# Autocorrelation on one core: weights transformed at plain delays, outputs as even and odd parts, and two steps moved

## What is computed

```python
qf, kf = fft(q), fft(k)
corr = ifft(qf * conj(kf)).real
w, idx = top_k(corr, topk)          # topk = int(2 ln 256) = 11
w = softmax(w)
for i in range(topk):
    g = minimum(idx[..., i] + pos, L - 1)
    out += w[..., i] * v[g]         # the context, shifted by the delay, clamped at its last row
```

## Time and profile before

| | |
|---|---|
| median of 3 runs | 2161.8 us (2161.77 to 2164.0) |
| profiled execution, its own time | 2167.1 us |
| profiled execution, span | 2165.1 us |
| mean granted TensorE clock | 0.977 |
| TensorE (PE) busy | 2052.2 us, 95% |
| VectorE (DVE) busy | 1098.7 us, 51% |
| ScalarE (ACT) busy | 1175.9 us, 54% |
| GpSimd (POOL) busy | 663.7 us, 31% |
| tail, from its first instruction | 1600.1 us to 2165.1 us |

### The profile page before, as it was taken

One profiled execution on the slowest core, in us unless ns is written; L12 is line 12 of the kernel. 1 busy time (PEld: TensorE's weight loads), 2 busy tenths in 40 slices (PEclk: granted clock), 3 DMA queues, 4 the chain that ended last, 5 costly groups with the idle time before them and its releaser, 6 DMA issues. The chain is left out here.

```text
span 2165.1 us, 25964 instructions
## 1 busy us (share of the span) xinstructions
PE 2052.2 (95%) x9634; PEld 1023.6 (47%) x9634; DVE 1098.7 (51%) x1951; ACT 1175.9 (54%) x1851; POOL 663.7 (31%) x640
## 2 busy tenths in 40 slices
PE   7985999999999999999999999999975899999997
PEld 5772444444444444444444444444432455555543
DVE  5774252442624335253352524335257788888852
ACT  6993755656566565665656566565613334344321
POOL 3432211112121121211112121121225676667741
PEclk9997999999999999999999999999987899999999
DMA  6632211112122121221221111111130011111000
GB/s 222 201 127 61 77 49 59 48 51 70 58 65 69 55 69 54 69 69 55 64 63 55 49 55 49 55 49 51 44 125 24 12 40 49 49 49 46 13 30 29
DMA packets 64925, 136.76 MB, mean 63 GB/s; under 512 B 8992, under 2 KB 13728, under 8 KB 64800
## 3 DMA queue, kind: packets, MB, share of 16 engines
q1 hardware_dynamic: 64800, 135.11, 19.1%
HBM read 122.49 MB, written 12.58 MB: 62 GB/s over the span
## 5 line engine op out<-in xcount | busy, mean ns | idle before, releaser
L682 ACT ACTIVATE first<-first 128x512 f32<-128x512 int32 x1008 | 632.7, 628 | 28.0
L920 PE MATMUL ps_ring<-xT_hi,gu_hi 128*128 128x512 f16 x1376 | 524.2, 381 | 1.7 <-POOL gu_lo L758 1.7
L920 PE MATMUL ps_ring<-xT_lo,gu_hi 128*128 128x512 f16 x1376 | 523.7, 381 | 0.0
L920 PE MATMUL ps_ring<-xT_hi,gu_lo 128*128 128x512 f16 x1376 | 523.2, 380 | 0.0
L812 DVE SCALAR_TENSOR_TENSOR wt<-first,w_scale,absm 128x512 f32<-128x512 f32 x132 | 98.8, 749 | 478.5 <-ACT first L682 477.4
L758 POOL TENSOR_TENSOR gu_lo<-wt,gu_hi 128x512 f16<-128x512 f32 x88 | 102.6, 1166 | 765.2 <-ACT gu_hi L688 765.2
L831 DVE SCALAR_TENSOR_TENSOR X<-ps_ring,ffn_gain,X 128x512 f32<-128x512 f32 x352 | 259.8, 749 | 135.3 <-PE ps_ring L943 135.3
L943 PE MATMUL ps_ring<-dn_hi,hid_hi 128*128 128x512 f16 x704 | 266.9, 379 | 0.0
L943 PE MATMUL ps_ring<-dn_hi,hid_lo 128*128 128x512 f16 x704 | 266.7, 379 | 0.0
L943 PE MATMUL ps_ring<-dn_lo,hid_hi 128*128 128x512 f16 x672 | 254.6, 379 | 0.0
L920 PEld LDWEIGHTS ps_ring<-xT_hi,gu_hi 128*128 128x128 f16 x1376 | 135.1, 98 | 171.7 <-issue 14.5
(11 more groups left out here) (203 smaller groups left out, 2683.1 us busy)
## 6 DMA issues: line engine op xcount, KB each, us to landing
first<-in_codes SPq DMA_DIRECT2D x132, 256.0 KB, 2.8
absm<-in_absmax SPq DMA_DIRECT2D x264, 128.0 KB, 3.0
X<-in_x SPq DMA_DIRECT2D x16, 512.0 KB, 4.3
c_in<-in_ctx SPq DMA_DIRECT2D x16, 512.0 KB, 5.3
cT<-in_ctxT SPq DMA_DIRECT2D x16, 512.0 KB, 3.6
xT_hi<-in_ctx SPq DMA_DIRECT2D x8, 1024.0 KB, 7.1
out<-X SPq DMA_DIRECT2D x16, 512.0 KB, 2.6
wide<-in_w SPq DMA_DIRECT2D x8, 512.0 KB, 4.7
```

Source lines behind the costliest of these rows:

```text
L682: act.activation(level[u % 2][:], codes[u % RING] if k == 0 else level[u % 2][:], ACT.Prelu, bias=bias, scale=scale, alpha=alpha).then_inc ...
L920: mm = pe.matmul(o[:], w[c][:, m, k, :], xx[:, k, ts], start=(q == 0), stop=(q == 3 * KD - 1))
```

## The change

The weights are no longer folded. `w_fold` goes; ScalarE norms `cut` itself, and both 128-delay halves of it are transposed. The transform matrices of the weights (`delay_hi`, `delay_lo`) take the 256 plain delays, so that each of the four spectra is a sum over both halves. The output is made as a symmetric part in `psQ[:, 0]` and an antisymmetric one in `psQ[:, 1]`. VectorE adds the symmetric part to both rows of X, ScalarE copies the antisymmetric one to SBUF, and GpSimd adds it to one row and subtracts it from the other. The moved steps are TensorE's `turn(nxt, 0)`, now behind `output(n)`, and VectorE's `add(n)`, now ahead of `low(nxt, 0)`. The list of ScalarE changes only where it is shown.

```diff
@@ SyncE, constants (in the feed-forward phase)
-                for name in ("fwd", "fwd_hi", "fwd_lo", "inv"):
+                for name in ("fwd", "fwd_hi", "fwd_lo", "inv", "back", "delay_hi", "delay_lo"):
                     sp.dma_start(res[name], io[name]).then_inc(res["const_in"], 16)
@@ GpSimd
-                def w_fold(n):
-                    if n:
-                        pool.wait_ge(wT_mm, n)
-                    for c in (0, 2):
-                        pool.wait_ge(w_done, CH * n + c + 2)
-                        for k, op in enumerate((ALU.add, ALU.subtract)):
-                            pool.tensor_tensor(wf[:, k, c:c + 2, :], cut[:, c:c + 2, 0:P], cut[:, c:c + 2, P:L][:, :, ::-1], op).then_inc(wf_done, 1)
+                def dc_fix(n):
+
+                    pool.wait_ge(wprod_comb, 4 * n + 1)
+                    pool.tensor_tensor(e_d[0:1, 0, :], e_d[0:1, 0, :], e_d[0:1, 1, :], ALU.subtract).then_inc(dc_done, 1)
+
+                def anti_add(n):
+                    pool.wait_ge(anti_done, n + 1)
+                    for t, op in enumerate((ALU.add, ALU.subtract)):
+                        pool.wait_ge(sym_done, 2 * n + t + 1)
+                        dst = X[:, 2 * (n // 2) + t, cols(n)]
+                        pool.tensor_tensor(dst, dst, anti[:], op).then_inc(x_done, 1)
...
                 for n in range(N + LAG):
                     now = tile(n - LAG)
+                    if 0 < n <= N:
+                        anti_add(n - 1)
                     if n + 1 < N:
                         corr_comb(n + 1)
...
                         out_comb(n, 1)
+                        dc_fix(n)
...
-                    if n + 1 < N:
-                        w_fold(n + 1)
@@ ScalarE
                 def weights(n):
                     act.wait_ge(rws_done, n + 1)
                     for c in range(CH):
-                        act.wait_ge(wf_done, 4 * n + 2 * (c // 2) + 2)
-                        act.activation(wf[:, :, c, :], wf[:, :, c, :], ACT.Copy, scale=rws[:, c:c + 1]).then_inc(wn_done, 1)
+                        act.activation(cut[:, c, :], cut[:, c, :], ACT.Copy, scale=rws[:, c:c + 1]).then_inc(wn_done, 1)
+
+                def anti_out(n):
+                    act.wait_ge(anti_mm, n + 1)
+                    if n:
+                        act.wait_ge(x_done, 2 * n)
+                    act.activation(anti[:], psQ[:, 1, :], ACT.Copy, scale=half_gate[:]).then_inc(anti_done, 1)
...
                         exps(n + 1)
                         odd_out(n + 1)
                         weights(n + 1)
+                    if n < N:
+                        anti_out(n)
                     if n + 2 < N:
                         even_out(n + 2)
@@ TensorE
                 def q_spectrum(n):
                     pe.wait_ge(qlo_done, n + 1)
                     if n >= 2:
-                        pe.wait_ge(x_done, 2 * n - 2)
+                        pe.wait_ge(sym_done, 2 * n - 2)
+                        pe.wait_ge(anti_done, n - 1)
...
+                def weight_spectrum(k):
+                    for half in range(2):
+                        for q, (w, src) in enumerate(((delay_hi, wT_hi), (delay_hi, wT_lo), (delay_lo, wT_hi))):
+                            for h in range(2):
+                                mm = pe.matmul(psE[:, half, :], w[:, 2 * k + half, h, :], src[:, h, :], start=(q + h == 0), stop=(q + h == 3))
+                    mm.then_inc(ws_mm, 1)
 
                 def weight_even(n):
...
-                    for half in range(2):
-                        mm = dft_parts(psE, half, half, wT_hi[:, half, :], wT_lo[:, half, :])
-                    mm.then_inc(ws_mm, 1)
+                    weight_spectrum(0)
...
                 def output(n):
                     pe.wait_ge(prod_done, min(2 * n + 4, 2 * N))
                     pe.wait_ge(wprod_row, n + 1)
-                    for k, src in enumerate((e_d, e_x, n_d, n_x)):
-                        pe.wait_ge(wprod_comb, 4 * n + k + 1)
-                        for t in range(2):
-                            mm = pe.matmul(psQ[:, t, :], inv[:, k, t * P:(t + 1) * P], src[:, 0, :], start=(k == 0), stop=(k == 3))
-                    mm.then_inc(out_mm, 1)
+                    pe.wait_ge(wprod_comb, 4 * n + 2)
+                    pe.matmul(psQ[:, 1, :], back[:, 1, :], e_x[:, 0, :], start=True, stop=False)
+                    pe.wait_ge(wprod_comb, 4 * n + 3)
+                    pe.matmul(psQ[:, 1, :], back[:, 2, :], n_d[:, 0, :], start=False, stop=True).then_inc(anti_mm, 1)
+                    pe.wait_ge(wprod_comb, 4 * n + 4)
+                    pe.matmul(psQ[:, 0, :], back[:, 3, :], n_x[:, 0, :], start=True, stop=False)
+                    pe.wait_ge(dc_done, n + 1)
+                    pe.matmul(psQ[:, 0, :], back[:, 0, :], e_d[:, 0, :], start=False, stop=True).then_inc(out_mm, 1)
...
                         linear(now, 1)
-                    if nxt is not None:
-                        turn(nxt, 0)
                     if n + 1 < N:
                         k_odd(n + 1)
                     if n < N:
                         output(n)
+                    if nxt is not None:
+                        turn(nxt, 0)
                     if n + 2 < N:
                         k_even(n + 2)
@@ VectorE
                     if n:
-                        dve.wait_ge(wf_done, 4 * n)
+                        dve.wait_ge(wT_mm, n)
...
                     for t in range(2):
                         dst = X[:, 2 * (n // 2) + t, cols(n)]
-                        dve.scalar_tensor_tensor(dst, psQ[:, t, :], half_gate[:], dst, ALU.mult, ALU.add).then_inc(x_done, 1)
+                        dve.scalar_tensor_tensor(dst, psQ[:, 0, :], half_gate[:], dst, ALU.mult, ALU.add).then_inc(sym_done, 1)
...
                         gain_of(now, 1)
+                    if n < N:
+                        add(n)
                     if nxt is not None:
                         low(nxt, 0)
-                    if n < N:
-                        add(n)
                     if nxt is not None:
                         low(nxt, 1)
```

More of the change, by code:

```diff
@@ L1015, in spectra @@
     fwd = np.stack([np.cos(even), even_im, np.cos(odd), -np.sin(odd)]).transpose(1, 0, 2)
-    scaled = fwd * DFT_SCALE
-    high = scaled.astype(np.float16)
+    weight = np.where(f == 0, 1.0, 2.0) / L
+    back_im = even_im * weight
+    back_im[:, :1] = np.sin(np.pi * t) / L
+    back = np.stack([np.cos(even) * weight, back_im, np.cos(odd) * 2 / L, -np.sin(odd) * 2 / L]).transpose(2, 0, 1)
     t = np.arange(L)[:, None]
@@ L1020, in spectra @@
     nyquist = np.where(t % 2 == 0, 1.0, -1.0)
-    weight = np.where(f == 0, 1.0, 2.0) / L
     im_inv = -np.sin(even) * weight
     im_inv[:, :1] = (nyquist - 1.0) / L
-    inv = np.stack([np.cos(even) * weight, im_inv, np.cos(odd) * 2 / L, -np.sin(odd) * 2 / L])
-    return fwd.astype(np.float32), high, (scaled - high).astype(np.float16), inv.transpose(2, 0, 1).astype(np.float32)
+    inv = np.stack([np.cos(even) * weight, im_inv]).transpose(2, 0, 1)
+    delay_im = -np.sin(even)
+    delay_im[:, :1] = -nyquist
+    delay = np.stack([np.cos(even), delay_im, np.cos(odd), -np.sin(odd)]).reshape(4, 2, P, P).transpose(2, 0, 1, 3)
+    scaled = [fwd[:, :2] * DFT_SCALE, delay * DFT_SCALE]
+    high = [m.astype(np.float16) for m in scaled]
+    low = [(m - h).astype(np.float16) for m, h in zip(scaled, high)]
+    return {"fwd": fwd.astype(np.float32), "inv": inv.astype(np.float32), "back": back.astype(np.float32),
+            "fwd_hi": high[0], "fwd_lo": low[0], "delay_hi": high[1], "delay_lo": low[1]}
 def phase_tail(nc, io, res):
@@ L1045, in sem @@
             return ctx.enter_context(nc.semaphore("a_" + name))
-        fwd, fwd_hi, fwd_lo, inv, const_in, ctx_in = (res[k] for k in ("fwd", "fwd_hi", "fwd_lo", "inv", "const_in", "ctx_in"))
+        fwd, fwd_hi, fwd_lo, inv, back, delay_hi, delay_lo = (res[k] for k in ("fwd", "fwd_hi", "fwd_lo", "inv", "back", "delay_hi", "delay_lo"))
+        const_in, ctx_in = res["const_in"], res["ctx_in"]
         c_in = [res[f"ctx_in{s}"] for s in range(2)]
@@ L1084, in phase_tail @@
         top_done, cut_done, nmax_done, next_done, fill_done, cut2_done = (sem(n) for n in ("top_done", "cut_done", "nmax_done", "next_done", "fill_done", "cut2_done"))
-        ex_done, w_done, rws_done, wf_done, wn_done = (sem(n) for n in ("ex_done", "w_done", "rws_done", "wf_done", "wn_done"))
+        ex_done, w_done, rws_done, wn_done = (sem(n) for n in ("ex_done", "w_done", "rws_done", "wn_done"))
         wT_mm, wT_done, ws_mm, wprod_done, wprod_comb, out_mm, x_done = (sem(n) for n in ("wT_mm", "wT_done", "ws_mm", "wprod_done", "wprod_comb", "out_mm", "x_done"))
-        wprod_row = sem("wprod_row")
+        wprod_row, dc_done, anti_mm, anti_done, sym_done = (sem(n) for n in ("wprod_row", "dc_done", "anti_mm", "anti_done", "sym_done"))
         l_stats, l_mv_done, l_ve_done, l_rstd_done, l_nmr_done, l_xn_done, T_mm, l_hi, l_lo, lin_mm, gained, added = (
```

(17 more changed lines are left out.)

9 lines of the change are left out of this document (3 added, 6 removed).

## The result

| | before | after |
|---|---|---|
| median of 4 runs | 2161.8 us (2160.6 to 2164.0) | 2220.0 us (2217.1 to 2222.4) |
| profiled execution, its own time | 2167.1 us | 2217.1 us |
| tail, from its first instruction to the end | 565.0 us | 620.0 us |
| eleven full turns (n = 3 to 13) | 328.5 us | 372.9 us |
| TensorE (PE) busy | 2052.2 us | 2054.8 us |

The changed kernel takes 1.027 times as long (95% interval 1.0257 to 1.0284). The tail begins at 1595.3 us in the profile after and at 1600.1 us in the one before; that difference of 4.8 us lies in the phases ahead of the change. Hence +55.0 us in the tail and only +50 us between the two profiled executions. In the medians it is +58.2 us.

What follows compares the result with a forecast made beforehand. TensorE, full in eleven turns, was taken as the bound; the change would open a gap there. Turn 2 +2, eleven turns +44.6, turn 14 +5.6, turn 15 +1.8 make +54 us: median 2161.8 to 2216 us, range 2199 to 2234.

Steps and rivals of the forecast that it cites:

- TensorE's own work: Per turn, weight transforms +2.59 us and output -3.43 us: -0.84 us, a turn of 28.97 us if nothing else bound.
- The moved turn and who queues behind it: On ScalarE, exps, odd_out, weights and anti_out wait behind high(nxt, 0); TensorE's k_even(n+2) gets a gap of 3.2 us.
- The clock in the gap: After the gap TensorE runs k_even at a lower clock, taking 3.4 us; the price is 1.7 us.
- The rival in which the clock holds: TensorE's clock stays full through the gap: +3.0 us a full turn, +40 in all, 2202 us; chance 15%.
- the one in which the slow level lasts longer: TensorE's low clock lasts into q_spectrum and the transpositions: 5.3 us a full turn, +69 in all, 2231 us; chance 15%.
- The ends: Turns outside the eleven full ones: 0 for turns 0 and 1, +2 turn 2, +5.6 turn 14, +1.8 turn 15.
- The median: The +54 us was added to the profiled 2167.1 us, giving 2221, and to the median 2161.8, giving 2216.
- GpSimd, cost 0: GpSimd loses 3.01 us of w_fold, gains two adds (2.5 us) and dc_fix (1.3 us), all covered: cost 0.
- The fast rival: TensorE stays the bound, with full turns of 28.97 us: -10 us, 2152 us; chance 4%.

Runs made afterwards that it cites:

- fold_held_anti_late: fold_held with GpSimd's anti_add(n-1) moved behind corr_comb(n+1): 2152.8 us, 0.9952 of the kernel before.
- turn_back: The changed kernel with turn(nxt, 0) back in its old place on TensorE, ahead of k_odd: 2180.0 us.
- exps_ahead: The changed kernel with exps(n+1) and odd_out(n+1) ahead of high(nxt, 0) on ScalarE: 2178.5 us.
- before_turn_late: The kernel before with only turn(nxt, 0) moved behind output(n) on TensorE: 2234.0 us.
- order_back: The changed kernel with turn(nxt, 0) back ahead of k_odd and add(n) back behind low(nxt, 0): 2175.0 us.
- fold_held: all_three with one wait added on GpSimd, so k_fold(n+3) starts only after VectorE's masked products: 2159.7 us.
- split_only: The changed kernel with VectorE's select cut in two, its maxima ahead of weight_products(n, 1): 2220.4 us.
- all_three: order_back with VectorE's select cut in two and ScalarE in the order exps, high, odd_out, anti_out, weights: 2169.2 us.

## Why the prediction was right

It said 2216 us (2199 to 2234) and slower; measured were 2220.0. Step by step:

| step | predicted | measured |
|---|---|---|
| wait of `high(nxt, 0)` | about 9 us | 10.0 |
| gap ahead of `k_even` | 3.2 us | 3.15 |
| `k_even` to next `weight_turn` | 5.15 us | 5.21 |
| `anti_out` | 0.60 (0.4 to 1.0) | 0.67 |
| `dc_fix` on one partition | 1.3 (0 to 1.3) | 1.26 |
| full turn | 33.85 us | 33.90 |
| eleven full turns | +44.6 us | +44.4 |
| tail up to turn 3 | +2 | +2.3 |
| turn 14 | +5.6 | +5.4 |
| turn 15 to the end | +1.8 | +2.9 |
| the tail | +54 | +55.0 |

- **TensorE's own work, -0.84 us.** Right to 0.1 us: a turn of 33.98 less the gap (3.15) and the clock's 5.21 - 3.45 = 1.76 is 29.07, and the turns without a gap in `fold_held_anti_late` take 28.90. The sum was 28.97.
- **The moved turn and who queues behind it.** Right, and shown from both sides: `turn_back` and `exps_ahead` remove it, and `before_turn_late` makes it in a kernel without the new arithmetic.
- **The clock in the gap.** Right in size for this kernel: 1.76 us lost for 1.7 taken, in ten turns of eleven. In the first of them `k_even` takes 3.44 us and the rest is at full speed, as I had it; later the slow level begins inside `k_even` and reaches into `q_spectrum`, at the same cost. In the last turn it does not come, and that turn takes 32.88 us, as the sum had it for a clock that holds (32.8); what TensorE waits for there is `low(nxt, 0)` (0.39 us, at the second transposition), not `anti_out`. The rival in which the clock holds (2202, 15%) and the one in which the slow level lasts longer (2231, 15%) are not what happened, though single turns of the first kind (n = 13 here) and of the second (`before_turn_late`) exist.
- **The ends.** +2.9 for +1.8 in turn 15 is the term that was sized too small. The clock behind the new gap is most of it: the first 24 matmuls of tile 13, behind gaps of 1.75 and 1.42 us, cost 1.7 us more than before where the sum had 1. The 24 behind turn 14's gap of 5.63 us cost 0.5 more, for which the sum had nothing, and `weight_odd` 1.75 for 1.4. The +2.3 up to turn 3 is right partly by chance: the sum had 0, 0 and +2 for turns 0, 1 and 2, and they came out at about +0.6, +0.7 and +1.0.
- **The median.** The sum stood against the profiled execution, and gave 2221 for it; it took 2217.1, since its phases ahead of the tail were 4.8 us shorter. The median of four runs is another 2.9 us above that. In the tail alone the error is 1.0 us in 55. Between the medians the rise is 58.2 us for 54; the other 3 us differ from one execution to the next, and no trace shows where.
- **GpSimd, cost 0.** Right here, and for the reason given: L1568 waits for `exps` anyway. The sentence that VectorE gets about 0.5 us back from the fold's going holds at that place: the four masked products went from 26.0 to 16.7 us in eleven turns, 0.85 us a turn. But the same contention with other instructions of GpSimd was not in the prediction, and it is worth 1.4 us a turn in the repaired kernels (30.66 to 29.29 by a wait and a move on GpSimd).
- **The fast rival.** I wrote that it would decide at `turn(nxt, 0)`, which had to come before about 20.5 us of the turn. That condition is too weak. `turn_back` and `order_back` have it there, and take 31.05 and 30.66 us, not 28.97. `order_back` meets the two others that I named as well: in the turn from 1852.90 `odd_out` ends at 24.3 us (before 25.44 was asked) and `weights` at 28.4 (before 28.9). With the new arithmetic the odd half of the products comes later on VectorE (in the kernel after and in `order_back` at 14.96 us of the turn, 12.43 before); `select` and `add` follow it, and `low(nxt, 0)` and `q_spectrum` wait for them (about 0.5 and 0.65 us of TensorE's idle time in each turn of `order_back`). The rival's number was reached within 1 us (2152.8 for 2152), but only with the lists of TensorE, ScalarE, VectorE and GpSimd all put in another order, and by chance: a full turn is 29.29, not 28.97, and the tail behind turn 13 gave 3.2 us where the rival had less than 1. That the longer chain on VectorE is the cause in `order_back` is read from its waits, and no run isolates it. A part of GpSimd's is in the same trace: the first instruction of `k_fix` took a mean of 1.36 us there, for 0.68 before, but TensorE waited for what stands behind it only 0.8 us in eleven turns.

## What to carry to other kernels

When a step is moved later on one engine, look for its reader on the next engine and count what stands behind that reader: in a list that runs in order, a single late input holds back everything that follows, needed or not. The repair may lie on either side, and moving the reader is as good as moving the writer. And when work is taken off the bottleneck, first see whether the other engines' chain became longer: here 0.84 us less on TensorE came out as 0.80 us more, and as 0.57 less only when three other engines had been put in a new order.

## What the runs showed of the hardware

**VectorE beside GpSimd.** In these traces a VectorE instruction with two inputs in SBUF does not share with a GpSimd instruction that runs; it waits until that has ended, and even for the next one if GpSimd has no pause: 0.41 us became 2.21 and 1.48, and `k_fix` 0.68 became 1.64. Small size is no shelter: `nmax`, 128x4 with one such input, took 1.95 us beside GpSimd's 2.13. The test is `fold_held` and its successor, in which no VectorE instruction was changed and the times fell where GpSimd was held back (1075 to 562 ns, and 1469 to 692). VectorE instructions that read PSUM (`low` at L1513 0.69, the products 1.22 of 128x1024) kept their times in all kernels, and so did MATCH_REPLACE8 with one large input. The Trainium skill (SBUF — State Buffer, Who interferes with whom) says that the port pair which the two engines share is an exclusive lock, and that a VectorE instruction contends for it when it has two SBUF inputs and GpSimd reads SBUF, or when it runs in a two-port mode, which `tensor_scalar` can enter. The rows of the masked products and of `k_fix` agree; whether `nmax` ran in such a mode no run shows. It also says, of the two-port modes, that the one who issues first has the pair for the whole instruction; the 2.21 us above show that a VectorE instruction which waits can lose to the next GpSimd instruction too.

**One partition is no cheaper.** GpSimd's `dc_fix` of 1x512 took 1.26 us, as the 128x512 of the same operation did (1.26 to 1.28).

**The clock and the length of a gap.** I had argued by the length of the gap alone. That does not decide. Of the kernel after, three turns from `k_even` to `weight_turn`, each behind a gap of 3.15 us:

```profile
1756.40:1761.60 5.20, 5.18 (x14) 2.40 (x15) 2.20 (x4) 3.53 (x7) 4.65 (x5) 0.67 0.25 101
...
2062.40:2067.60 5.20, 5.20 (x14) 2.28 (x15) 3.30 (x6) 3.57 (x7) 3.77 (x3) 0.67 0.26 102
2096.40:2100.50 4.10, 3.70 (x14) 1.78 (x15) 2.66 (x5) 3.62 (x7) 3.27 (x3) 1.00 0.32 128
```

Ten turns have a mean granted clock of 0.67 there, partly 1.2 GHz, and the last one stays at 1.00 and is 1.1 us shorter. `split_only` has three such turns of eleven, and in the turn behind each of them `k_even` starts at 0.50:

```profile
1929.50:1933.50 4.00, 3.61 (x14) 1.73 (x15) 2.56 (x5) 3.58 (x7) 3.20 (x3) 1.00 0.32 131
1962.40:1965.80 3.40, 3.40 (x4) 1.33 (x5) 2.25 (x4) 2.05 (x5) 2.82 (x4) 0.50 0.26 105
```

In `turn_back` nine gaps of 1.8 us left the clock at its full level, and the one of 2.10 us did not:

```profile
1910.70:1915.10 4.40, 4.35 (x19) 2.74 (x20) 2.63 (x4) 1.21 (x2) 2.27 (x2) 0.61 0.29 119
```

And in `all_three` two short gaps, of 1.20 and 0.65 us, cost the clock once, where two like pairs in its other turns did not (1.00 in the same stretch at 1846.6 and 1970.1):

```profile
1784.10:1789.00 4.90, 4.19 (x18) 2.88 (x19) 4.21 (x6) 1.85 (x4) 3.16 (x3) 0.70 0.26 107
```

What decides besides the length stays open; no run was made for it.
